# Constant products inside TensorE's waits, in a four-stage transformer kernel

## The chip, the cores and the metric

The kernel runs on one core of a Trainium2 chip. The metric is the device time of one execution in microseconds. Engines are named as in the profile: PE is TensorE (PEld its weight loads), DVE is VectorE, ACT is ScalarE, POOL is GpSimd, SP is SyncE, which issues DMAs.

## The reference

A batch of 8 sequences of 256 rows of 256 numbers runs through four residual layers, each on a layer-normalised input, each weighted by a tanh gate:

1. Cross attention to 120 context rows, 16 heads of 16 (`softmax(q k / 4) v`, then an output projection), with a padding mask.
2. "Mixture attention": 16 heads of 64 attend over the 256 rows. Values and output projection come from 8 experts, of which a gate picks 2 for each head and row.
3. Cross attention again, other weights, with an additive mask of 256 x 120.
4. A mixture of 12 experts with 3 chosen for each row: `gelu(x Wup + bup) Wdown + bdown`, hidden size 1024, summed with softmaxed gate weights.

## The kernel before, in words

Everything is computed to nearly fp32 precision: a number is split into a high and a low fp16 part, and a product is three fp16 products (hi·hi, hi·lo, lo·hi) that add up in PSUM, which is `matmul3` (lines 77 to 85, so most PE rows of the profile carry L82, L83 or L84). Every engine has its program written out in order; semaphores tie them. There are six blocks one after the other (setup, attention 1, mixture attention, attention 2, route, experts), and each ends for all engines before the next begins.

In an attention block (`xattn_stage`) a batch has five front parts, each in the one "front" bank of PSUM: transpose the rows (XN_T, line 517), transpose the context (CTX_T, line 522), project queries (Q_T), keys (K_T) and values (V_). ACT and DVE bring each part to SBUF (high part, then low part), and PE's next part waits for the bank (`front_done`). After that the batch has 8 units of 4 heads: PE scores (a mask product of 128x480 on line 547, in attention 2 three more for the additive mask on line 545, then six products on 32 rows on line 550), DVE maxima, ACT exponentials, PE transposes (line 560), ACT and DVE split them, PE multiplies with V. In the loop the front parts of the next batch stand between the units of this one, and the work on finished rows of the batch before (lines 581, 587, 590) as well. For batch 0 the five front parts stand alone ahead of the loop, and its first two units directly behind them.

The mixture attention (`ffn_stage`) is built in the same way: 16 front parts in two banks, in the order FF_ORDER, alone for batch 0; then 16 heads per batch. After the heads of a batch, ACT and DVE write the head outputs, SP sends them to DRAM and back in another layout, DVE spreads the gate masks, and PE mixes the experts (`mixed_back`, 64 products on line 1208) and multiplies with the output weights (`back_product`). For the last batch nothing is left beside that: the loop's last round, b = B, is this tail.

In the route (`route`) PE transposes the rows, computes gate scores, waits for DVE's choice, ranks and counts (lines 1690 to 1695), transposes gate weights, builds a table of slots from one-hot products (line 1709) and in between the bias term (`base_part`, line 1670), whose last parts wait for DVE. The experts (`run_experts`) begin with two transposes of gathered rows (`turn_rows`, line 1910) and the first up projection (`up(0, 0, 0)`), and go on with 35 blocks.

The lines below are those ahead of which the change puts something: line 595 (`project(0, j)` in the attention), 1221 (the same in the mixture), the two calls at MIX_STEPS and PRODUCT_STEPS, the waits for `masks_made` and `sel_ready` in the route, the end of the route, and `up(0, 0, 0)`.

Of the kernel before, what the change touches and what calls it, by code (L numbers as in the profile page):

```python
# [25 lines left out]
P = 128  # L26
# [9 lines left out]
B, SQ, D = 8, 256, 256  # L36
# [41 lines left out]
def matmul3(pe, out, terms):  # L78

    last = None  # L80
    for n, (lhs, rhs) in enumerate(terms):
        pe.matmul(out, lhs[0], rhs[0], start=(n == 0), stop=False)  # L82
        pe.matmul(out, lhs[0], rhs[1], start=False, stop=False)  # L83
        last = pe.matmul(out, lhs[1], rhs[0], start=False, stop=(n == len(terms) - 1))  # L84
    return last


def rsqrt_all(dve, chain, s):
# [252 lines left out]
ROWS32 = 32  # L341
HG = 4
BACK = 2 * TPB


def xattn_stage(nc, a, s, layer):
# [3 lines left out]
    with ExitStack() as ctx:  # L350
# [24 lines left out]
        ps = ctx.enter_context(nc.psum_tensor(t + "ps", [P, 8, 512], F32))  # L375
# [131 lines left out]
        def _(pe):  # L507
# [84 lines left out]
                last.then_inc(back_ready, 1)  # L592

            for j in range(XA_FRONT):
                project(0, j)
            pe.wait_ge(ones_set, 4)
            score(0, 0)
# [22 lines left out]
        def _(dve):  # L620
# [129 lines left out]
F_XN, F_GATES, F_PV, F_Q, F_K, F_MIXV = "xn", "gates", "pv", "q", "k", "v"  # L750
FF_ORDER = ((F_XN, 0), (F_GATES, 0), (F_PV, 0), (F_PV, 1), (F_Q, 0), (F_K, 0), (F_Q, 1), (F_K, 1), (F_Q, 2), (F_K, 2),
            (F_Q, 3), (F_MIXV, 0), (F_MIXV, 1), (F_MIXV, 2), (F_MIXV, 3), (F_K, 3))
# [3 lines left out]
MIX_STEPS, SPLIT_STEPS, PRODUCT_STEPS, UPDATE_STEPS = [9, 12], [10, 13], [11, 14], [12, 15]  # L756
F_Z, F_OUT = "z", "out"
LOW_KINDS = (F_PV, F_Q, F_K, F_MIXV)


def bank_uses():
# [36 lines left out]
def ffn_stage(nc, a, s):  # L798
# [7 lines left out]
    with ExitStack() as ctx:  # L806
# [293 lines left out]
        def _(pe):  # L1100
# [112 lines left out]
            def back_product(b, ti):  # L1213
                out = open_bank((b, (F_OUT, ti)))
                pe.wait_ge(z_done, TPB * b + ti + 1)
                matmul3(pe, out[:, 0:D],
                        [(tuple(zt[:, hl, ec, :] for hl in range(2)), tuple(s.fo[:, hl, ec, :] for hl in range(2)))
                         for ec in range(E0 // 2)]).then_inc(front_ready, 1)

            for j in range(FF_FRONT):  # L1220
                project(0, j)
            score(0, 0)
            score(0, 1)
            for b in range(B + 1):
                for h in range(H):
                    earlier(b, h, 1, transposes)
                    earlier(b, h, FF_LAG, times_v)
                    if b < B - 1:
                        project(b + 1, h)
                    if b < B and h + 2 < H:  # L1230
                        score(b, h + 2)
                    elif b < B - 1 and h + 2 >= H:
                        score(b + 1, h + 2 - H)
                    for ti in range(TPB):
                        if b >= 1 and h == MIX_STEPS[ti]:
                            mixed_back(b - 1, ti)
                        if b >= 1 and h == PRODUCT_STEPS[ti]:
                            back_product(b - 1, ti)

        @block.vector  # L1240
# [181 lines left out]
UP_PAIRS = M // 2  # L1422
# [120 lines left out]
def route(nc, s, t, sem, ps, xt, xg, rows_in, row_of, expert_of, weights, ident16, out):  # L1543
# [14 lines left out]
    with ExitStack() as prep:  # L1558
# [95 lines left out]
        @block.tensor  # L1654
        def _(pe):
            def gate(k):
                pe.wait_ge(tr_done, k + 1)
                for ti in range(TPB):
                    last = matmul3(pe, G[:, TPB * k + ti, :],
                                   [(tuple(xt[k % 2][:, hl, c, ti * P:(ti + 1) * P] for hl in range(2)),  # L1660
                                     tuple(s.wg[:, hl, c, :] for hl in range(2))) for c in range(C)])
                last.then_inc(gate_done, 1)

            def base_part(q):
                pe.wait_ge(cwt_done, 3 if q == 3 else q // 2 + 1)
                if BASE_BANKS[q] in BASE_BANKS[:q]:
                    pe.wait_ge(b_done, BASE_BANKS.index(BASE_BANKS[q]) + 1)
                for ti in range(TPB):
                    tile = TPB * q + ti
                    last = pe.matmul(BASE(q)[:, ti, :], cwt[:, tile * P:(tile + 1) * P], s.bdown[:], start=True, stop=True)  # L1670
                last.then_inc(b_ready, 1)

            pe.wait_ge(masks_made, 1)
            for k in range(B):
                pe.wait_ge(xn_split, k + 1)
                if k >= 2:
                    pe.wait_ge(tr_done, k - 1)
                for hl in range(2):
                    for c in range(C):
                        for ti in range(TPB):  # L1680
                            at = (hl * C + c) * SQ + ti * P
                            last = pe.transpose(tr(k)[:, at:at + P], limbs[:, TPB * k + ti, hl, c * P:(c + 1) * P], ident16[:])
                last.then_inc(tr_ready, 1)
                if k >= 1:
                    gate(k - 1)
            gate(B - 1)

            pe.wait_ge(masks_made, 6)
            pe.wait_ge(sel_ready, 1)
            pe.matmul(RANK, before[:], sel16[:], start=True, stop=False)  # L1690
            for tile in range(TILES - 1):
                pe.matmul(RANK[:, tile + 1:, :], ones[:], bcast_mid(sel16[:, tile, :], TILES - 1 - tile),
                          start=False, stop=(tile == TILES - 2))
            for tile in range(TILES):
                last = pe.matmul(TOTAL, ones[:], sel16[:, tile, :], start=(tile == 0), stop=(tile == TILES - 1))
            last.then_inc(counted, 1)
            pe.wait_ge(cw_ready, 1)
            for q in range(TILES // 4):
                if q >= 2:
                    pe.wait_ge(cwt_done, q - 1)  # L1700
                for ti in range(4):
                    last = pe.transpose(CW_T(q)[:, ti * P:(ti + 1) * P], cw_out[:, 4 * q + ti, :], s.ident[:])
                last.then_inc(cwt_ready, 1)
            for q in range(BASE_AHEAD):
                base_part(q)
            for n in range(CHOICES):
                if n % TILES == 0:
                    pe.wait_ge(hot_ready, n // TILES + 1)
                last = pe.matmul(MAP, lane_hot[:, n, :], column_hot[:, n, :], start=(n == 0), stop=(n == CHOICES - 1))
            last.then_inc(map_ready, 1)  # L1710
            for q in range(BASE_AHEAD, B):
                base_part(q)

        def lo_part(dve, k):
            tiles = slice(TPB * k, TPB * k + TPB)
# [89 lines left out]
def run_experts(nc, s, t, sem, ctx, ps, xg, xt, rows_in, row_of, ident16, out, weights):  # L1805
# [89 lines left out]
    @block.tensor  # L1895
    def _(pe):
        pe.sem_inc(u_ready, 2 * UP_PAIRS)
        pe.sem_inc(y_ready, 2 * TPB)
        pe.sem_inc(turned, 2)

        def turn_rows(j, par, turn):
            pe.wait_ge(x_loaded[j % RING], 16 * TPB * (j // RING + 1))
            if j >= 1:
                pe.wait_ge(xt_split, j)
            rows = xg[j % RING][:].bitcast(F16)
            for hl in range(2):
                for c in range(C):
                    for ti in range(TPB):
                        at = (hl * C + c) * BT + ti * P
                        last = pe.transpose(T[:, at:at + P], rows[:, ti, hl * D + c * P:hl * D + (c + 1) * P], ident16[:])  # L1910
            last.then_inc(turned, 1)

        def up(j, par, turn):
            pe.wait_ge(up_split, 2 + j + 1)
            pe.wait_ge(xt_split, j + 1)
            for q in range(UP_PAIRS):
                pe.wait_ge(h_gelu, UP_PAIRS * j + q + 1)
                for m in (2 * q, 2 * q + 1):
                    last = matmul3(pe, U(q)[:, m % 2, :],
                                   [(tuple(weights.us[par][:, hl, k, m * P:(m + 1) * P] for hl in range(2)),  # L1920
                                     tuple(xt[par][:, hl, k, :] for hl in range(2))) for k in range(C)])
                last.then_inc(u_ready, 1)

        def down(j, par, turn):
            pe.wait_ge(h_done, UP_PAIRS * (j + 2))
            pe.wait_ge(down_split, 2 + j + 1)
            for ti in range(TPB):
                pe.wait_ge(y_done, TPB * j + ti + 1)
                matmul3(pe, Y(ti),
                        [(tuple(hs[par][:, hl, m, ti * P:(ti + 1) * P] for hl in range(2)),  # L1930
                          tuple(weights.dsp[par][:, hl, m, :] for hl in range(2))) for m in range(M)]).then_inc(y_ready, 1)

        turn_rows(0, 0, 0)
        turn_rows(1, 1, 0)
        up(0, 0, 0)

        def slot(j, par, turn):
            ahead(j, par, turn, 1, up)
            ahead(j, par, turn, 2, turn_rows)
            down(j, par, turn)  # L1940

        for j in range(NB):
            slot(j, j % 2, j // 2)
# [131 lines left out]
```

## Time and profile before

| | us |
|---|---|
| three timed runs | 1438.38, 1441.53, 1442.84 |
| median | 1441.53 |
| span of the profiled execution | 1442.0 |
| PE busy | 1253.7 (87%) |
| PE weight loads | 996.9 (69%) |
| DVE busy | 1135.6 (79%) |
| ACT busy | 903.7 (63%) |
| mean granted clock of TensorE | 0.919 of full speed |

Busy time is the share of the span in which an engine had an instruction under way. The granted clock has two levels: 1.00 is 2.4 GHz, 0.50 is 1.2 GHz, and a number between them is a stretch that holds both. A row of a timeline gives start and duration in us, engine, line and operation, what it writes and reads, and in brackets how long the engine stood idle before it and what ended that. Matmuls are pipelined: a row's duration is longer than the distance to the next row. The stages lie in the span thus: setup to 48.7 us, attention 1 to 255.9, mixture attention to 751, attention 2 to 982.6, route to 1040, experts to the end.

### The profile page before, as it was taken

The page shows a single profiled execution, that of the slowest core. Times are in us where ns is not written, and L with a number is a line of the kernel's source. Part 1 is how long each engine was busy: PE and PEld are TensorE (multiplying, and loading weights), DVE is VectorE, ACT ScalarE, POOL GpSimd, SP SyncE. Part 2 cuts the span into 40 slices and gives each one's busy share as a digit, 9 for nine tenths or more (in the row PEclk, how much of TensorE's full clock was granted, in tenths as well). Part 3 has the DMA queues.
Part 4 walks back from the last instruction along what each step waited for, and adds up shares of the span by engine and source line. Part 5 has one row for each costly group of instructions (what it writes and reads, how often), then busy time and mean ns, then how long its engine had stood idle before and what let it go on. Part 6 is the DMA issues. An engine that isn't in the chain of part 4 may idle for free. (4 is left out here: it accounts for less than half of the span.)

```text
span 1442.0 us, 35263 instructions
## 1 busy us (share of the span) xinstructions
PE 1253.7 (87%) x13822; PEld 996.9 (69%) x13822; DVE 1135.6 (79%) x2068; ACT 903.7 (63%) x2071; POOL 278.4 (19%) x242
## 2 busy tenths in 40 slices
PE   1599998589989899889938999994699999999996
PEld 1376666367767767667725676763489999899995
DVE  5578887689999999999643777777688888888884
ACT  1477875158667677667624667663277677677762
POOL 2000000100000000000000000000236666666663
PEclk8689999799999999999666999995599999999998
DMA  8000000133452353352220000000867788778871
GB/s 231 12 9 9 6 2 2 41 93 74 114 146 67 101 151 76 100 151 73 68 66 9 5 9 5 2 2 1 290 225 227 227 249 245 222 231 250 234 189 30
DMA packets 172065, 152.96 MB, mean 106 GB/s; under 512 B 62589, under 2 KB 154386, under 8 KB 171906
## 3 DMA queue, kind: packets, MB, share of 16 engines
q1 hardware_dynamic: 151906, 129.51, 30.0%
q0 software_dynamic: 13936, 16.79, 6.1%
q10 hardware_dynamic: 6064, 4.46, 1.1%
q8 instruction: 110, 1.80, 0.5%
q14 instruction: 49, 0.40, 0.1%
HBM read 116.89 MB, written 36.70 MB: 107 GB/s over the span
## 5 line engine op out<-in xcount | busy, mean ns | idle before, releaser
L1857 POOL DMA_INDIRECT out<-m_yo,m_xg x70 | 161.5, 2307 | 135.9 <-DVE m_yo L1972 120.5
L1879 ACT ACTIVATE m_hf<-m_ps,m_bue 128x256 f32<-128x256 f32 x280 | 117.3, 471 | 106.5 <-PE m_ps L84 106.5
L82 PE MATMUL m_ps<-m_xt,m_us 128*128 128x256 f16 x560 | 153.7, 274 | 0.0
L83 PE MATMUL m_ps<-m_xt,m_us 128*128 128x256 f16 x560 | 153.7, 274 | 0.0
L84 PE MATMUL m_ps<-m_xt,m_us 128*128 128x256 f16 x560 | 153.6, 274 | 0.0
L82 PE MATMUL m_ps<-m_ds,m_hs 128*128 128x256 f16 x560 | 152.6, 273 | 0.3 <-DVE m_yo L1972 0.3
L84 PE MATMUL m_ps<-m_ds,m_hs 128*128 128x256 f16 x560 | 152.6, 273 | 0.0
L83 PE MATMUL m_ps<-m_ds,m_hs 128*128 128x256 f16 x560 | 152.6, 273 | 0.0
L473 ACT ACTIVATE x_pr<-x_ps,x_mx 128x120 f32<-128x120 f32 x512 | 143.3, 375 | 9.8 <-DVE x_mx L687 9.2
L1053 ACT ACTIVATE f_pr<-f_ps,f_nb 128x256 f32<-128x256 f32 x256 | 107.8, 477 | 66.0 <-DVE f_nb L1331 65.7
L481 ACT ACTIVATE x_pt<-x_ps 120x512 f16<-120x512 f32 x128 | 77.0, 602 | 86.2 <-PE x_ps L84 78.8
L691 DVE SCALAR_TENSOR_TENSOR x_pt<-x_ps,x_pt 120x512 f16<-120x512 f32 x128 | 88.2, 689 | 54.2 <-ACT x_pt L481 53.2
L1539 DVE SCALAR_TENSOR_TENSOR m_ds<-m_draw,m_ds 128x2048 f16<-128x2048 f32 x35 | 80.2, 2292 | 42.7 <-ACT m_ds L1527 42.7
L550 PE MATMUL x_ps<-x_km,x_qt 32*128 32x240 f16 x768 | 105.9, 273 | 0.0
L1335 DVE SCALAR_TENSOR_TENSOR f_pt<-f_ps,f_pt 128x512 f16<-128x512 f32 x128 | 87.5, 684 | 19.9 <-ACT f_pt L1023 19.8
L1962 DVE SCALAR_TENSOR_TENSOR m_hs<-m_hf,m_hs 128x512 f16<-128x512 f32 x140 | 96.9, 692 | 4.8
L550 PEld LDWEIGHTS x_ps<-x_km,x_qt 32*128 32x128 f16 x768 | 63.6, 96 | 53.0 <-issue 46.3
L1486 POOL DMA_INDIRECT m_xg<-expert_in,m_row_of x70 | 83.2, 1189 | 69.6 <-DVE m_row_of L1796 40.8
L82 PE MATMUL f_ps<-f_kt,f_qt 64*128 64x256 f16 x256 | 72.0, 282 | 25.5 <-ACT f_pr L1053 25.3
L1023 ACT ACTIVATE f_pt<-f_ps 128x512 f16<-128x512 f32 x128 | 79.0, 617 | 23.7 <-PE f_ps L84 23.5
L687 DVE TENSOR_REDUCE x_mx<-x_ps 128x4 f32<-128x480 f32 x128 | 83.5, 653 | 12.3 <-PE x_ps L550 9.8
L1331 DVE TENSOR_REDUCE f_nb<-f_ps 128x2 f32<-128x512 f32 x128 | 87.6, 685 | 2.0 <-PE f_ps L84 0.7
(367 smaller groups left out, 3832.7 us busy)
## 6 DMA issues: line engine op xcount, KB each, us to landing
m_uraw<-in_L_ffn_Wup SPq DMA_DIRECT2D x35, 1024.0 KB, 5.5
m_draw<-in_L_ffn_Wdown SPq DMA_DIRECT2D x35, 1024.0 KB, 5.8
head_values<-f_v_row SPq DMA_DIRECT2D x16, 520.0 KB, 5.5
f_vh<-head_values SPq DMA_DIRECT2D x16, 520.0 KB, 3.9
head_outputs<-f_at_row SPq DMA_DIRECT2D x16, 512.0 KB, 3.0
f_at_in_t<-head_outputs SPq DMA_DIRECT2D x16, 512.0 KB, 6.1
expert_values<-f_pv_row SPq DMA_DIRECT2D x8, 512.0 KB, 2.8
f_pv_in_t<-expert_values SPq DMA_DIRECT2D x8, 512.0 KB, 5.6
```

The source lines that it names most:

```text
L82: pe.matmul(out, lhs[0], rhs[0], start=(n == 0), stop=False)
L83: pe.matmul(out, lhs[0], rhs[1], start=False, stop=False)
L84: last = pe.matmul(out, lhs[1], rhs[0], start=False, stop=(n == len(terms) - 1))
L473: ins = act.activation(pr[u % 2][:, h, :], S(u)[:, h, :], ACT.Exp, bias=mx[u % 2][:, h:h + 1])
L550: last = pe.matmul(S(u)[:, 2 * m:2 * m + 2, :], qt[par][rows, ql, m, ti * P:ti * P + P], km[par][rows, kl, m, :, :], start=False, stop=(m ...
L691: dve.scalar_tensor_tensor(pt[u % 2][:, 1], PT(u), SPLIT, pt[u % 2][:, 0], ALU.mult, ALU.subtract).then_inc(pt_done, 1)
L1053: ins = act.activation(pr[h % 2][:, ti, :], S(h)[:, ti, :], ACT.Exp, bias=nb[h % 2][:, ti:ti + 1])
L1331: dve.tensor_reduce(nb[h % 2][:], S(h), AX_X, ALU.max, negate=True).then_inc(s_max, 1)
L1335: dve.scalar_tensor_tensor(pt[h % 2][:, 1].rearrange("p c t q -> p (c t q)"), PT(h), SPLIT, pt[h % 2][:, 0].rearrange("p c t q -> p (c t q)"),
L1857: pool.indirect_dma_start(rows_of, bass.IndirectOffsetOnAxis(xg[j % RING][:, ti, D:D + 1].bitcast(I32), 0), yo[j % 2][:, ti, :], None, bou ...
L1879: ins = act.activation(hf[:, q, m, :], U(q)[:, m, :], ACT.Gelu, bias=weights.bue[par][:, 2 * q + m:2 * q + m + 1], scale=UNSPLIT)
L1962: dve.scalar_tensor_tensor(hs[par][:, 1, 2 * q:2 * q + 2, :], hf[:, q], SPLIT, hs[par][:, 0, 2 * q:2 * q + 2, :], ALU.mult, ALU.subtract). ...
```

## The change

A helper issues `n` products of 128x512 fp16 elements of the mixture attention's query weights with a 128x128 piece of the same weights, into a bank of PSUM that nothing reads before it is written anew. They wait for nothing and tell no semaphore. The helper is called ahead of each front part of batch 0 in both attentions and of four parts in the mixture attention, three times in the mixture's last round (`b == B`), twice in the route and once in the experts: 153 products in all. At the route's end a wait for `map_done` goes ahead of them, because their bank held the slot table.

```diff
+def idle_products(pe, s, bank, n):
+    for _ in range(n):
+        pe.matmul(bank, s.fq[:, 0, 0, 0:P], s.fq[:, 0, 0, 0:512], start=True, stop=True)
...
+XA_IDLE = (3, 5, 2, 6, 4)
...
             for j in range(XA_FRONT):
+                idle_products(pe, s, ps[:, 7, :], XA_IDLE[j])
                 project(0, j)
...
+FF_IDLE = {(F_XN, 0): 2, (F_GATES, 0): 4, (F_K, 0): 3, (F_MIXV, 0): 14}
...
             for j in range(FF_FRONT):
+                idle_products(pe, s, ps[:, 7, :], FF_IDLE.get(FF_ORDER[j], 0))
                 project(0, j)
...
                         if b >= 1 and h == MIX_STEPS[ti]:
+                            if b == B and ti == 0:
+                                idle_products(pe, s, ps[:, 2, :], 40)
                             mixed_back(b - 1, ti)
                         if b >= 1 and h == PRODUCT_STEPS[ti]:
+                            if b == B:
+                                idle_products(pe, s, ps[:, 2, :], 4)
                             back_product(b - 1, ti)
...
             gate(B - 1)
+            idle_products(pe, s, ps[:, 7, :], 20)
             pe.wait_ge(masks_made, 6)
             pe.wait_ge(sel_ready, 1)
...
             for q in range(BASE_AHEAD, B):
                 base_part(q)
+            pe.wait_ge(map_done, 1)
+            idle_products(pe, s, ps[:, 7, :], 16)
...
         turn_rows(0, 0, 0)
         turn_rows(1, 1, 0)
+        idle_products(pe, s, ps[:, UP_PAIRS + 2, :], 6)
         up(0, 0, 0)
```

PE's order at the start of attention 1, before the change (x_xn are the rows, x_ctx the context, x_ps the attention's PSUM):

```order
L506 UNCONDITIONAL_BRANCH
L517 MATMUL x_ps<-ident,x_xn 128x128 x4
L522 MATMUL x_ps<-ident,x_ctx 128x120 x2
L82 MATMUL x_ps<-x_xt,w_q 128x256
L83 MATMUL x_ps<-x_xt,w_q 128x256
```

And with the change (lines below the helper are numbered 6 or 7 higher; fq are the constant weights):

```order
L513 UNCONDITIONAL_BRANCH
L91 MATMUL x_ps<-fq 128x512 x3
L524 MATMUL x_ps<-ident,x_xn 128x128 x4
L91 MATMUL x_ps<-fq 128x512 x5
L529 MATMUL x_ps<-ident,x_ctx 128x120 x2
L91 MATMUL x_ps<-fq 128x512 x2
L82 MATMUL x_ps<-x_xt,w_q 128x256
L83 MATMUL x_ps<-x_xt,w_q 128x256
```

Nothing has changed places; the constant products stand between two parts, ahead of the wait of the second. The start of attention 2 reads the same.

PE's order in the tail of the mixture attention with the change, from the last product with values (f_vh) on; before it, the same rows stand without those of L91:

```order
L84 MATMUL f_ps<-f_vh,f_pt 128x65
L91 MATMUL f_ps<-fq 128x512 x40
L1217 MATMUL f_ps<-f_spread_z,f_at_in_t 64x4x16 x64
L91 MATMUL f_ps<-fq 128x512 x4
L82 MATMUL f_ps<-fo,f_zt 128x256
```

The 40 follow the last head directly, ahead of the mixing's waits for the masks and for the head outputs; 4 stand between each mixing and the output product that waits for its split.

PE's order from the slot table (m_lane_hot) over the route's end into the experts, with the change; the two branches end one block and begin the next:

```order
L1724 MATMUL m_ps<-m_ds,m_lane_hot 128x70 x48
L1684 MATMUL m_ps<-bdown,m_cwt 128x256 x8
L91 MATMUL m_ps<-fq 128x512 x16
L1572 UNCONDITIONAL_BRANCH
L1912 UNCONDITIONAL_BRANCH
L1927 MATMUL m_ps<-m_ident,m_xg 128x128 x16
L91 MATMUL m_ps<-fq 128x512 x6
L82 MATMUL m_ps<-m_xt,m_us 128x256
```

Sixteen are the last that PE does in the route; six stand between the two row turns (x16 together) and the first up projection.

## Rows read from the trace of the kernel before

**Rows 1.** Stretches: us, busy time and instructions of each engine, granted clock (PEclk), DMA.
```profile
58.20:61.60 3.40, 0.80 (x12) 0.64 (x12) 0.69 (x1) 1.78 (x6) 0.00 (x0) 1.00 0.00 0
61.70:82.10 20.40, 19.61 (x99) 12.40 (x100) 9.69 (x20) 10.38 (x30) 0.00 (x0) 0.50 0.03 8
686.30:706.50 20.20, 19.89 (x138) 14.20 (x137) 13.20 (x20) 13.14 (x33) 0.00 (x0) 0.50 0.40 112
713.00:724.90 11.90, 10.49 (x202) 9.17 (x200) 8.84 (x19) 8.45 (x26) 0.00 (x0) 1.00 0.01 1
735.80:744.30 8.50, 6.45 (x140) 5.15 (x140) 1.78 (x4) 1.09 (x2) 0.00 (x0) 0.50 0.12 32
751.10:785.20 34.10, 25.51 (x104) 14.52 (x105) 11.09 (x27) 9.86 (x27) 1.19 (x6) 0.50 0.08 17
796.60:947.40 150.80, 150.80 (x1585) 106.74 (x1584) 112.52 (x246) 104.23 (x313) 0.00 (x0) 1.00 0.02 5
1040.00:1048.10 8.10, 6.30 (x37) 4.80 (x38) 3.13 (x4) 4.17 (x5) 3.00 (x2) 0.50 0.84 310
...
37.80:44.50 6.70, 4.26 (x31) 3.04 (x29) 1.00 0.00 0
```
**Rows 2.** Stretches, line 1183 alone (128x512 products): us, PE, PEld, clock, DMA.
```profile
302.00:303.60 1.60, 1.46 (x6) 0.54 (x6) 1.00 0.03 3
307.20:309.90 2.70, 2.60 (x6) 0.71 (x6) 0.54 0.00 0
```
**Rows 3.** Stretches, tile x_xt alone: query projections of batch 0 and 1.
```profile
55.00:58.00 3.00, 2.74 (x12) 1.64 (x12) 0.00 (x0) 0.00 (x0) 0.50 0.19 52
97.80:99.40 1.60, 1.47 (x12) 1.10 (x12) 0.00 (x0) 0.00 (x0) 1.00 0.33 90
```
**Rows 4.** Timeline of PE, front of attention 1: start, us, instruction, idle before.
```profile
53.52 0.66 PE L522 MATMUL x_ps<-ident,x_ctx 120*128 120x120 f32 x2 [2.63 <-DVE x_xt L656]
55.09 0.39 PE L82 MATMUL x_ps<-x_xt,w_q 128*128 128x256 f16 x1 [0.91 <-DVE x_ct L660]
...
60.22 0.23 PE L82 MATMUL x_ps<-x_ct,w_k 128*128 128x120 f16 x1 [2.39 <-DVE x_qt L665]
```
**Rows 5.** Timeline of PE, first units of batches 0, 1, 2, both attentions.
```profile
63.85 0.58 PE L547 MATMUL x_ps<-x_mb,mask_w 128*128 128x480 bf16 x1
...
88.03 0.36 PE L547 MATMUL x_ps<-x_mb,mask_w 128*128 128x480 bf16 x1 [0.20 <-ACT x_pr L473]
...
110.49 0.36 PE L547 MATMUL x_ps<-x_mb,mask_w 128*128 128x480 bf16 x1 [0.43 <-ACT x_pr L473]
...
768.08 0.61 PE L547 MATMUL x_ps<-x_mb,mask_w 128*128 128x480 bf16 x1
...
796.57 0.36 PE L547 MATMUL x_ps<-x_mb,mask_w 128*128 128x480 bf16 x1
...
821.71 0.36 PE L547 MATMUL x_ps<-x_mb,mask_w 128*128 128x480 bf16 x1
```
**Rows 6.** Timeline of PE, front of the mixture: gate projection, first value products.
```profile
259.86 0.39 PE L82 MATMUL f_ps<-fg,f_xt 128*128 128x256 f16 x1 [1.91 <-DVE f_xt L1273]
...
287.07 0.23 PE L82 MATMUL f_ps<-f_pv_in_t,f_spread_v 128*128 128x64 f16 x1 [5.30 <-DVE f_spread_v L1304]
```
**Rows 7.** Timeline of PE, tail of the mixture: first mixing, first output product.
```profile
735.77 0.45 PE L1208 MATMUL f_ps<-f_spread_z,f_at_in_t 128*64 128x64 f16 x9 [10.82 <-issue]
...
739.20 0.37 PE L82 MATMUL f_ps<-fo,f_zt 128*128 128x256 f16 x1 [1.50 <-DVE f_zt L1348]
```
**Rows 8.** Stretches, line 1208 alone: a mixing at either clock.
```profile
715.50:716.80 1.30, 1.20 (x64) 1.09 (x64) 1.00 0.00 0
735.70:737.80 2.10, 1.92 (x64) 1.82 (x64) 0.50 0.54 145
```
**Rows 9.** Timeline of PE: ranking in the route, first row turn of the experts.
```profile
1007.86 0.32 PE L1690 MATMUL m_ps<-m_sel,m_before 128*128 128x192 f16 x1 [8.26 <-DVE m_sel L1752]
...
1040.60 0.69 PE L1910 MATMUL m_ps<-m_ident,m_xg 128*128 128x128 f16 x5 [7.64 <-PEq L1558]
```

## The prediction

> **What bounds the kernel now.** I read the granted clock first, stretch by stretch, then the products that stand on both sides of a clock change, then the waits of TensorE. The first view splits the span into stretches at TensorE's upper level (2.4 GHz, shown as 1.00) and at its lower one (1.2 GHz, shown as 0.50) [rows 1]. The reader is to see two kinds of low stretch. In 61.7–82.1, 686.3–706.5 and 768–785 PE is busy nearly all the time at 0.50: there the clock is the limit. In the others (the fronts of the stages, the tail of the mixture attention, the start of the experts) PE mostly waits, and its short bursts run at 0.50 and stand on the chain between two waits. The same product at both levels gives the price of a level: six of 128x512 take 1.46 us at 1.00 and 2.60 at 0.54 [rows 2], so one costs 0.22 to 0.24 us high and 0.43 low; the twelve products of a query projection take 1.47 against 2.74 [rows 3]. The third view shows what ends PE's waits: evacuations by DVE in the fronts, 2.63, 0.91 and 2.39 us long in the first attention [rows 4], and larger ones further on [rows 6 to 8].
>
> **The change part by part.** It takes nothing away and moves no wait. It adds 153 products of 128x512 on 128 rows, each ahead of a wait of PE. Each costs nothing where it ends before its wait does; what it can give is a high clock for what follows.
>
> First batch of attention 1. In PE's order stand 3, 5, 2, 6 and 4 products ahead of the five parts. At the low price 5 take 2.13 us against the 2.63 of wait, 2 take 0.85 against 0.91, 6 take 2.56 against 2.39, or 1.3 if the clock has risen [rows 2, 4]. So they fit. With the real work between, PE is nearly never idle from the stage's first wait to the query projection. In the trace the clock was high from 58.2 on, right after the 12 query products had run without a break, and fell again when PE was busy 0.80 of the next 3.40 us [rows 1]. I take it as high before the query projection: 2.74 becomes 1.47, −1.27 on the chain. Then the units. From the first unit of batch 0 to the first of batch 1 it is 24.18 us, from there to batch 2 22.46 [rows 5], although batch 0 has none of the work on finished rows. At the high clock batch 0 takes no more than a steady batch, −1.7; the bounds are 0 (the clock falls as before) and half of PE's 19.61 busy us at 0.50, −9.8 [rows 1], which ACT and DVE will not allow. I take −1.7, the end next to a row, because the first units wait for exponentials and their scores run on 32 rows: the clock may fall there. Attention 1: −3.0.
>
> Front of the mixture. The gate projection is again 12 products of 256 columns after a wait of 1.91 us, which 4 low products (1.7) fill [rows 2, 6]: −1.27. The first value products follow a wait of 5.30 us [rows 6]; 14 products take 3.1 us high, 6.0 low (0.7 too long). The 48 value products that ran at 0.50 there would go from some 3.2 us (287.1 to 290.3 in the trace) to about half, −1.4, but DVE's spreads stand between them. The 2 ahead of the transposes and the 3 ahead of the first keys last 0.9 and 1.3 us at most, low; if no wait covered them they would cost that, +2.2. Of +2.2 to −2.7 I take −2.0: the first term whole, the second by half.
>
> Tail of the mixture. 40 products go into the wait of 10.82 us ahead of the last mixing [rows 7]. The clock is high just before (713–724.9, [rows 1]), so they take 8.8 us and end 2 us before the wait does. Behind them, the 64 mixing products take 1.20 us instead of 1.92, twice [rows 8], and the twelve of the output 1.47 instead of 2.74, with 4 products (0.9) inside the 1.50 us wait [rows 3, 7]: −0.72·2 −1.27 = −2.7, all of it on the chain, since nothing else runs. If the clock is low when they start they take 17.2 us: 6.4 too long.
>
> First batch of attention 2. The front has the same five waits, and its query and key products both ran low (751.1–785.2 is at 0.50 throughout, [rows 1]): −1.27, and for the key's 12 products of 120 columns, by columns, 0.6. The units: 28.49 us for batch 0, 25.14 for batch 1 [rows 5]. In the steady batches PE is busy 150.80 of 150.80 us at 1.00 [rows 1], so PE's work alone sets the pace, and here every unit holds three more full-width products of 128 rows (line 545) than in attention 1, enough to keep PE busy from the first unit on. As long as a steady batch: −3.35. At most half of PE's busy time from 768.1 to 785.2 comes back, −8.5. Batch 0 lacks the work on finished rows and the tail of a batch before, so I go well past the first bound: −7.0. Attention 2: −8.9.
>
> Route and experts. 20 products precede the ranking, after a wait of 8.26 us [rows 9]: 8.6 low, 4.9 high, and the clock rises on the way; DVE is at other work until after the totals anyway. 16 more follow at PE's end of the route, in 7.64 us of idle before the experts [rows 9]; 6.9 low, so they fit. In the experts' start PE is busy 6.30 of 8.10 us at 0.50 [rows 1]. Half of that comes back, −3.15, but the 6 products ahead of the first up projection stand behind row turns whose next step waits for nothing, so they are paid in full, 1.3: −1.85. If the clock is low there they cost 2.6 and give nothing. From there PE runs without a break, so whatever is won stays won.
>
> Sum: −3.0 −2.0 −2.7 −8.9 −1.85 = −18.5 on the profiled span of 1442.0, 1423.5. The median of the runs shown is 1441.53, 0.5 less: 1423.
>
> **A rule against the row.** Much of the first units is fp32 transposes. In 37.8–44.5 the clock is 1.00, and all that PE had done before and does in it is transposes of line 247 [rows 1]. So they do raise it. The Trainium skill, "TensorE: Matmul & The Clock Gate", section "Part 4: PE-mode transpose", says that transposes do not count as PE activity for the clock in the same way. By that rule the first batches would lose the clock between projections, and the sum would be that of case (a); the trace speaks against it.
> The same page, section "Back-to-back issue gap", gives some 0.13 us per 512-column product in a stream. An estimate by it: the 40 products would end 5.6 us before the tail's wait does, long enough for the clock to fall as it did in the trace, and 2.7 us of the sum would go (1426). The row shows 0.22 to 0.24 [rows 2], and by the row only 2 us stay open.
>
> **The rivals.** (a) The fronts speed up but the clock does not hold through the units of either first batch, as it did not in 61.7–82.1, where PE was busy 19.61 of 20.40 us at 0.50 [rows 1]: being busy alone did not raise it there, with 32-row scores and fp32 transposes (that transposes alone are to blame has 0.03 of this case's chance). Left are −1.27, −2.0, −2.7, −1.9, −1.85 = −9.7: 1432. Against it for attention 2: the same mixture holds 1.00 for 150 us.
> (b) Nothing changes: the waits are set by DVE, ACT and DMAs, and bursts that end earlier only wait longer. For it: every wait of rows 4 is ended by DVE. Against it: the evacuations wait for PE in turn. 1441.
> (c) Slower: constant operands do not raise the clock, and all 153 products run at 0.43. Its place is the tail, 17.2 us in a wait of 10.82: +6.4; then 2.6 ahead of the experts, 0.7 at the value products, 0.2 each at the two output products. +10: 1452. It decides from the point where the 40 products take over 0.27 us each. For it: at 686.3–706.5 PE is busy all along at 0.50, 20 us before the tail, and if that stretch lies later the tail starts low. Against it: the mixing before the tail brought the clock back in the trace.
>
> **How the numbers follow.** Forecast 0.68; (a) 0.17; (b) 0.07; (c) 0.08. Each end has a few us of luck in where the clock falls: between the two ends of the units' gain the forecast case alone runs from 1414 to 1430. The 8-in-10 range takes in (a): 1413 to 1435. A measurement here tells about 0.3% (4.3 us) from no change. Faster by more than that: the forecast, (a) and little else, 0.85; within: 0.08; slower: 0.07.
>
> **What would show it.** In the profile after: the query projections of both attentions in 1.5 us; the first batch of attention 2 in 20 to 22 us at clock 1.00 (wrong if 28); that of attention 1 in 21 to 23, and in 24 if its clock falls; the 40 products of 0.22 us each, over before the last mixing starts, which takes 1.2; the first up projection at 1.00 from its start, 0.4 us later than now after the row turns. The prediction fails if the first batch of attention 2 stays at 0.50, or if the last mixing follows the 40 products without a wait.

## The result and the profile after

The changed kernel takes 1422.24 us (median of 4 runs, 1418.0 to 1424.71) against 1440.12 (4 runs, 1438.38 to 1442.84): ratio 0.9872, 95% interval 0.9845 to 0.99. Measured a second time it was 1420.31 against 1440.12, ratio 0.9862 (0.9837 to 0.9887). The profiled execution has a span of 1423.0 us where before had 1442.0.

The page of the kernel after, engine totals: the added products make PE busier, and the span is shorter all the same.

```profile
span 1423.0 us, 35569 instructions
...
PE 1272.8 (89%) x13975; PEld 1001.2 (70%) x13975; DVE 1135.9 (80%) x2068; ACT 903.0 (63%) x2071; POOL 280.4 (20%) x242
```

Stretches of the kernel after (us, busy time and instructions of PE, PEld, DVE, ACT, POOL, granted clock, DMA), the counterpart of [rows 1]:

```profile
51.60:65.20 13.60, 9.40 (x64) 5.21 (x63) 5.93 (x16) 4.94 (x14) 0.00 (x0) 1.00 0.06 16
65.30:75.50 10.20, 10.20 (x45) 6.26 (x44) 4.05 (x7) 5.33 (x17) 0.00 (x0) 0.50 0.05 14
174.60:181.30 6.70, 6.70 (x51) 4.83 (x50) 5.18 (x13) 3.96 (x12) 0.00 (x0) 0.50 0.00 0
281.00:283.70 2.70, 0.63 (x22) 0.63 (x23) 1.91 (x3) 0.00 (x0) 0.00 (x0) 1.00 0.05 4
283.80:293.90 10.10, 8.23 (x99) 6.46 (x97) 5.86 (x7) 2.99 (x5) 0.00 (x0) 0.50 0.27 63
...
734.30:737.60 3.30, 3.30 (x14) 1.61 (x12) 0.69 (x1) 0.36 (x1) 0.00 (x0) 0.50 0.00 0
760.90:781.50 20.60, 20.60 (x189) 13.55 (x188) 13.39 (x27) 14.59 (x44) 0.00 (x0) 1.00 0.03 9
1021.10:1038.60 17.50, 14.47 (x128) 11.57 (x127) 10.01 (x13) 10.68 (x18) 3.01 (x2) 1.00 0.63 224
```

Attention 2's first batch is at 1.00 from end to end, and so is the start of the experts. Attention 1's first batch begins at 1.00 and falls at 65.3, in the units. Two places of the mixture behind added products are at 0.50 as well: the value products behind 281.0–283.7, where PE worked 0.63 of 2.70 us, and an output product of the tail.

Timeline of PE in the kernel after, the front of attention 1 (start, us, instruction, idle before), against [rows 4]:

```profile
48.80 1.44 PE L91 MATMUL x_ps<-fq 128*128 128x512 f16 x3 [4.49 <-PEq L138]
...
50.88 1.61 PE L91 MATMUL x_ps<-fq 128*128 128x512 f16 x5
53.58 0.43 PE L529 MATMUL x_ps<-ident,x_ctx 120*128 120x120 f32 x2 [1.08 <-DVE x_xt L664]
53.84 0.60 PE L91 MATMUL x_ps<-fq 128*128 128x512 f16 x2
54.91 0.28 PE L82 MATMUL x_ps<-x_xt,w_q 128*128 128x256 f16 x1 [0.47 <-DVE x_ct L668]
...
56.23 1.46 PE L91 MATMUL x_ps<-fq 128*128 128x512 f16 x6
58.78 0.23 PE L82 MATMUL x_ps<-x_ct,w_k 128*128 128x120 f16 x1 [1.09 <-DVE x_qt L673]
```

Four of the five groups end before their wait does: 1.08, 0.47 and 1.09 us of idle remain of 2.63, 0.91 and 2.39, and 0.60 of 1.47 ahead of the value projection. The first group doesn't: DVE had the rows ready at 49.68 (49.66 before the change), and the transposes follow the 3 products without idle at 50.03, where they began at 49.81; some 0.2 us are lost there. The query products last from 54.91 to the 6 constant ones at 56.23.

First units of batches 0, 1 and 2 in both attentions, kernel after, against [rows 5]:

```profile
62.41 0.36 PE L554 MATMUL x_ps<-x_mb,mask_w 128*128 128x480 bf16 x1 [0.49 <-issue]
83.73 0.36 PE L554 MATMUL x_ps<-x_mb,mask_w 128*128 128x480 bf16 x1 [0.21 <-ACT x_pr L480]
106.18 0.36 PE L554 MATMUL x_ps<-x_mb,mask_w 128*128 128x480 bf16 x1 [0.42 <-ACT x_pr L480]
...
760.92 0.36 PE L554 MATMUL x_ps<-x_mb,mask_w 128*128 128x480 bf16 x1
781.52 0.36 PE L554 MATMUL x_ps<-x_mb,mask_w 128*128 128x480 bf16 x1
806.66 0.36 PE L554 MATMUL x_ps<-x_mb,mask_w 128*128 128x480 bf16 x1
```

Batch 0 takes 21.32 us in attention 1 (before 24.18) and 20.60 in attention 2 (before 28.49), less than the next batches with 22.45 and 25.14.

The mixture's tail and the start of the experts, kernel after, against [rows 7, 9]:

```profile
721.72 8.80 PE L91 MATMUL f_ps<-fq 128*128 128x512 f16 x40
732.82 1.20 PE L1217 MATMUL f_ps<-f_spread_z,f_at_in_t 128*64 128x64 f16 x64 [2.30 <-issue]
733.95 1.61 PE L91 MATMUL f_ps<-fq 128*128 128x512 f16 x4
735.53 0.37 PE L82 MATMUL f_ps<-fo,f_zt 128*128 128x256 f16 x1
...
737.97 1.20 PE L1217 MATMUL f_ps<-f_spread_z,f_at_in_t 128*64 128x64 f16 x64
739.10 1.04 PE L91 MATMUL f_ps<-fq 128*128 128x512 f16 x4
740.75 0.27 PE L82 MATMUL f_ps<-fo,f_zt 128*128 128x256 f16 x1 [0.61 <-DVE f_zt L1362]
...
1024.41 0.61 PE L1927 MATMUL m_ps<-m_ident,m_xg 128*128 128x128 f16 x8 [1.83 <-PEq L1572]
1026.22 0.61 PE L1927 MATMUL m_ps<-m_ident,m_xg 128*128 128x128 f16 x8 [1.21 <-ACT m_xt L1889]
1026.67 1.46 PE L91 MATMUL m_ps<-fq 128*128 128x512 f16 x6
1027.96 0.27 PE L82 MATMUL m_ps<-m_xt,m_us 128*128 128x256 f16 x1
```

The 40 take 0.22 us each and leave 2.30 us of the wait. Both mixings take 1.20, but the first output product runs from 735.53 to 737.97, since the clock is at 0.50 there.

Where the time went, from such rows in two profiles of each kernel. A line is the length of a stretch, from start to start; "the other batches" run to the last mask product, and the last head, the tail and the up products are counted to the end of their last product.

| stretch | before | again | after | again |
|---|---|---|---|---|
| start to attention 1's first mask product | 63.85 | 63.75 | 62.41 | 61.83 |
| attention 1, batch 0 | 24.18 | 24.14 | 21.33 | 21.45 |
| attention 1, the other batches | 150.28 | 150.21 | 152.72 | 150.23 |
| mixture, row transposes to the seventh head's scores | 56.46 | 56.24 | 55.13 | 55.08 |
| mixture, fifth to last head of the last batch | 35.46 | 33.57 | 34.01 | 34.65 |
| mixture, tail after the last values | 21.86 | 21.62 | 20.33 | 19.24 |
| attention 2, row transposes to first mask product | 16.00 | 15.52 | 13.23 | 13.11 |
| attention 2, batch 0 | 28.49 | 28.40 | 20.61 | 20.60 |
| attention 2, the other batches | 170.01 | 169.98 | 170.00 | 169.98 |
| route to first row turn | 55.23 | 55.12 | 54.94 | 54.57 |
| first row turn to first up product | 3.02 | 3.02 | 3.55 | 3.55 |
| first 96 up products | 12.84 | 12.44 | 10.64 | 10.64 |

Attention 2's two lines hold 10.65 of the 19.0 us between the first profiles.

### The profile page after: what moved, and what is told of

Read it like the earlier page. It is cut to its first block and busy times, and to the rows that moved or that the text cites. A ratio compares the mean times of both kernels' runs of the same rounds, so it can differ in the third digit from the quotient of the medians.

```text
span 1423.0 us, 35569 instructions
## 1 busy us (share of the span) xinstructions
PE 1272.8 (89%) x13975; PEld 1001.2 (70%) x13975; DVE 1135.9 (80%) x2068; ACT 903.0 (63%) x2071; POOL 280.4 (20%) x242
## 5 line engine op out<-in xcount | busy, mean ns | idle before, releaser
L557 PE MATMUL x_ps<-x_km,x_qt 32*128 32x240 f16 x768 | 102.6, 267 | 0.0
```

What stands on the lines that cost most here:

```text
L557: last = pe.matmul(S(u)[:, 2 * m:2 * m + 2, :], qt[par][rows, ql, m, ti * P:ti * P + P], km[par][rows, kl, m, :, :], start=False, stop=(m ...
```

## The experiments

My theory: what a group is worth is the level of the clock in the work behind it, and what raises the level is how much of the array works. Rivals: any unbroken work of PE would do, or the groups lean on each other. The edits are to the changed kernel, except that of `attention2_alone`, which adds the helper and one group to the kernel before. `after_again`, `before_again` and the second execution of `without_attention2` run a kernel once more as it was. Every stage is read from one profile of each run.

**Attention 2's products alone** (`attention2_alone`).

```diff
+XA_IDLE = (3, 5, 2, 6, 4)
...
             for j in range(XA_FRONT):
+                if layer == 1:
+                    idle_products(pe, s, ps[:, 7, :], XA_IDLE[j])
                 project(0, j)
```

> Only the 20 products of the second attention are left; the other 133 and the wait for map_done are out. Theory (each group is worth what the higher clock gives to the work behind it, and the groups add): from the first transposes of attention 2 to its first mask product 13.2 us (before 16.0), batch 0 20.6 us (before 28.5), so 10.6 us under the kernel before: 1429.5. The mixture's tail and the start of the experts stay as before. Rival (the groups lean on each other, a stage starts high only because the one before it ended high): attention 2 stays at 0.50 or gains at most the projections, 1437 or more.

1427.58 us against 1441.08, ratio 0.9906 (0.9881 to 0.9932). Its first batch of attention 2, 763.13 to 783.74:

```profile
763.10:783.70 20.60, 20.60 (x189) 13.55 (x188) 13.38 (x27) 14.57 (x44) 0.00 (x0) 1.00 0.03 8
```

13.40 us of front and 20.61 of batch 0, as forecast, although the mixture's tail ahead of it stayed at 21.64. The group stands on its own; the rival falls. The median is 13.5 us lower where these two stretches give 10.5; the runs reach from 1424.96 to 1433.04.

**All but attention 2's** (`without_attention2`, and the same kernel once more).

```diff
-                idle_products(pe, s, ps[:, 7, :], XA_IDLE[j])
+                if layer == 0:
+                    idle_products(pe, s, ps[:, 7, :], XA_IDLE[j])
```

> The changed kernel without the 20 products of attention 2. Theory (the groups add): attention 2 as before the change, 16.0 us of front and 28.5 us of batch 0 at 0.50, so 10.7 us over the changed kernel: 1433. Rival (the work before, or the better tail of the mixture, brings the clock up anyway): batch 0 of attention 2 under 24 us and 1426 or less.

1426.28 us against 1441.08 (1420.98 to 1430.81), ratio 0.9904 (0.9883 to 0.9926). That is 4 to 6 us over the changed kernel (its two medians), not 10.7. In the profile the front of attention 2 ran low and took 15.86 us, but batch 0 took 21.09, at a mean clock of 0.97: it came up about 1 us after the first units began.

```profile
755.90:777.00 21.10, 21.10 (x189) 13.66 (x188) 13.50 (x27) 14.56 (x44) 0.00 (x0) 0.97 0.04 9
```

So:

> The changed kernel without attention 2's products, a second time: in the first profile batch 0 of attention 2 took 21.1 us, its clock up from the first units though its front ran at 0.50. Theory (at 0.50 these units lie at the edge, and what the clock does is settled anew in each execution): another value this time, up to 28.5 us. Rival (the groups ahead of attention 2 bring this about): 21.1 us again.

The stretches of that second execution, from the end of the front on:

```profile
754.70:771.70 17.00, 15.25 (x55) 7.80 (x56) 6.83 (x16) 6.36 (x19) 0.00 (x0) 0.50 0.03 9
771.80:788.20 16.40, 16.40 (x173) 11.36 (x170) 11.01 (x22) 11.90 (x35) 0.00 (x0) 1.00 0.01 2
```

Here batch 0 began at 758.97, stayed low until 771.8 and took 26.54 us (one run, 1431.11). The same program, the same stage: 21.09 and 26.54. So attention 2 can get part of the gain without its own products. Front and batch 0 together took 36.95 and 41.89 us against 33.84 in the changed kernel, 3.1 and 8.1 more, mean 5.6, near the 4 to 6 us of the medians; two executions don't tell how often either happens.

**The kernel before, again** (`before_again`).

> The kernel before a second time, for its first batches. Theory (below the edge it stays low every time): attention 1's batch 0 24.2 us, attention 2's 28.5 us, the first up projections 12.8 us. Rival (the clock comes up by itself in some executions): one of them at least 3 us shorter.

1439.81 us (one run). Batch 0 24.14 and 28.40, the up products 12.44; in attention 2:

```profile
761.30:781.60 20.30, 19.12 (x72) 10.49 (x73) 8.13 (x18) 6.45 (x18) 0.00 (x0) 0.50 0.03 8
```

Low again. Attention 2's batch 0 took 20.60 or 20.61 us in all eight profiles with 128-row products ahead of it. Without them it ran low for some 17 us in both profiles of before and in `rows32`, and for 13 us or 1 in those of `without_attention2`. Whether that difference is chance or comes from the groups ahead stays open; three against two executions don't settle it.

**The same products on 32 rows** (`rows32`).

```diff
-        pe.matmul(bank, s.fq[:, 0, 0, 0:P], s.fq[:, 0, 0, 0:512], start=True, stop=True)
+        pe.matmul(bank, s.fq[0:32, 0, 0, 0:P], s.fq[0:32, 0, 0, 0:512], start=True, stop=True)
```

> The same 153 products with operands on 32 of the 128 rows: the same columns and the same number of instructions, in the same places. Theory (what counts is how much of the array works, so that PE busy with 32 rows does not bring the clock up): attention 2 stays at 0.50, batch 0 takes 28 us, the first up projections 12.8; the products fill waits and gain nothing, and those that do not fit cost up to 5 us: 1440 to 1446. Rival (any unbroken work of PE brings the clock up): as the changed kernel, 1422, with batch 0 of attention 2 in 20.6 us at 1.00.

1450.44 us against 1441.08, ratio 1.0058 (1.0037 to 1.0079): 9 us slower than before, and 28 to 30 over the kernel with the same instructions on 128 rows. The stretches of the mixture's front, of the tail, of attention 2's front (two) and of its first units, and two rows of the tail:

```profile
267.00:290.80 23.80, 16.62 (x113) 10.14 (x111) 15.89 (x24) 6.04 (x11) 2.35 (x6) 1.00 0.26 61
727.80:748.20 20.40, 20.40 (x157) 9.10 (x155) 6.34 (x8) 1.77 (x3) 0.00 (x0) 0.50 0.33 104
755.10:765.30 10.20, 9.29 (x30) 3.73 (x30) 2.56 (x10) 1.26 (x3) 1.28 (x6) 0.50 0.18 41
765.40:768.70 3.30, 2.52 (x21) 1.24 (x20) 0.69 (x1) 1.68 (x6) 0.00 (x0) 1.00 0.00 0
768.80:789.20 20.40, 19.67 (x74) 10.51 (x73) 8.17 (x18) 6.46 (x19) 0.00 (x0) 0.50 0.03 8
```

```profile
725.61 15.12 PE L91 MATMUL f_ps<-fq 32*128 32x512 f16 x40
740.66 1.92 PE L1217 MATMUL f_ps<-f_spread_z,f_at_in_t 128*64 128x64 f16 x64
```

In 727.8–748.2, the 40 products and the tail behind them, PE worked 20.40 of 20.40 us and stayed at 0.50; in the front of attention 2, 9.29 of 10.20 and the same. From 765.4 to 768.7, behind the query projection, the clock was up, and then low again through the first units; the front of `before_again` does this without any added product (757.8–761.1 at 1.00). So PE busy nearly all along with products on 32 rows didn't bring attention 2's batch 0 up, which took 28.38 us; any unbroken work of PE is not enough. The clock even fell under the 40 products, which began at 1.00: they took 15.12 us and the tail 26.09 (+4.2). With the row turns (+2.8), attention 1's batch 0 (25.72, +1.5) and its other batches (152.76, +2.5) that is more than I had forecast. One stretch doesn't fit "gain nothing": the mixture's front took 54.28 us, 2.0 to 2.2 less than the 56.24 to 56.46 without products, its clock up from 267.0 to 290.8, where before it fell under the first keys (269.9–273.2 at 0.50). With 128 rows it took 52.70 to 55.13. What the 32 rows did there, one profile doesn't settle. Only 32 and 128 rows were run, on the same weights: that the share of the array at work decides is read from these two points.

**One late group** (`late12`).

```diff
+                idle_products(pe, s, ps[:, 7, :], (XA_IDLE, (0, 0, 0, 0, 12))[layer][j])
```

> In attention 2 alone the five groups (3, 5, 2, 6, 4) become one of 12, ahead of the value projection; all else as in the changed kernel. Theory (the units need only a high clock at their start and then hold it themselves): the front goes back to 0.50 and 16 us, and the 12 products, 5.1 us at 0.43, outlast the wait of 1.9 us by up to 3.2; but batch 0 takes 20.6 us at 1.00: 1426 to 1429. Rival (the units need the whole front high): batch 0 stays near 28.5 us at 0.50 and the 3.2 us are lost: 1436 to 1439.

1423.54 us against 1441.08, ratio 0.989 (0.9856 to 0.9925).

```profile
752.96 3.85 PE L91 MATMUL x_ps<-fq 128*128 128x512 f16 x12
...
757.31 0.77 PE L552 MATMUL x_ps<-causal_b,ident_b 128*128 128x480 bf16 x3
```

```profile
741.60:755.00 13.40, 7.70 (x35) 4.58 (x36) 3.22 (x8) 3.14 (x8) 0.45 (x3) 0.50 0.13 31
755.20:778.50 23.30, 23.30 (x205) 15.15 (x204) 14.35 (x29) 15.69 (x46) 0.00 (x0) 1.00 0.03 8
62.40:79.80 17.40, 16.14 (x165) 11.54 (x165) 12.97 (x26) 14.11 (x44) 0.00 (x0) 1.00 0.04 9
```

The front takes 16.25 us (+3.0), batch 0 of attention 2 20.61: a clock that is high at the start of the units is enough, and they hold it. (In `without_attention2` it was low at their start and came up a little later.) Twelve products in one place give 7.6 of attention 2's 10.65 us. The median lies 2.5 us below the forecast. In the profiled execution attention 1 also held its clock (last line), and its batch 0 took 17.39 us; the runs reach from 1418.79 to 1434.71, and the others aren't profiled.

**The changed kernel again** (`after_again`).

> The changed kernel a second time, unaltered, for what differs between executions of one program. Theory (where the clock is raised by a margin it comes up every time, and where the work itself is near the edge it differs): attention 2's batch 0 again in 20.6 us; attention 1's batch 0 in 17.4 us if the clock holds through its units and 21.3 if it falls as in the first profile; 1418 to 1425. Rival (the clock follows the program alone): every stage within 0.3 us of the first profile.

1420.31 us against 1440.12, ratio 0.9862 (0.9837 to 0.9887). Attention 2 within 0.12 us in both lines; attention 1's clock fell again, at 63.3, 1.5 us behind the first mask product where it was 2.9 in the first profile:

```profile
61.80:63.20 1.40, 1.38 (x9) 0.72 (x10) 0.98 (x3) 0.00 (x0) 0.00 (x0) 1.00 0.00 0
63.30:73.50 10.20, 10.20 (x45) 6.53 (x44) 5.44 (x11) 5.17 (x16) 0.00 (x0) 0.50 0.05 14
```

The tail was 19.24 us this time, with its output product at 1.00, and attention 1's other batches 150.23 for 152.72. So stretches of one program differ by 1 to 2.5 us between these two executions; attention 2's first batch no longer does.

**Without the six** (`no_six`).

```diff
-        idle_products(pe, s, ps[:, UP_PAIRS + 2, :], 6)
```

> The changed kernel without the 6 products ahead of the first up projection. Theory (the 16 products at the end of the route have raised the clock already, and the 6 are paid in full): the first 96 up products still take 10.6 us at 1.00 and start 1.1 to 1.4 us sooner after the second row turn: 1421. Rival (the clock falls in the two waits around the row turns without them): 12.8 us as before the change, 1424.

1420.2 us against 1440.12, ratio 0.9857 (0.9831 to 0.9883); the timing can't tell it from the changed kernel, the trace can:

```profile
1022.21 0.61 PE L1927 MATMUL m_ps<-m_ident,m_xg 128*128 128x128 f16 x8 [1.91 <-PEq L1572]
1024.02 0.61 PE L1927 MATMUL m_ps<-m_ident,m_xg 128*128 128x128 f16 x8 [1.21 <-ACT m_xt L1889]
1024.46 0.27 PE L82 MATMUL m_ps<-m_xt,m_us 128*128 128x256 f16 x1
```

From the first row turn to the first up product 2.25 us (with the six 3.55), and the 96 up products take 10.64 either way. The 16 at the end of the route had raised the clock; the six cost 1.3 us and gave nothing.

**The last batch of the mixture** (`last_batch`). Two products for each of seven heads, at the place where the clock fell in every profile so far. `bank_left` makes PE wait until the bank's last contents have been read.

```diff
+            def last_idle(b, h):
+                if b == B - 1 and 2 <= h <= 8:
+                    bank_left((b, FF_ORDER[-1]))
+                    idle_products(pe, s, bank((b, FF_ORDER[-1])), 1)
...
+                    last_idle(b, h)
                     earlier(b, h, FF_LAG, times_v)
+                    last_idle(b, h)
```

> The changed kernel with two more constant products for each of seven heads (h = 2 to 8) in the mixture's last batch, where the clock fell to 0.50 for 17 us in the profile after and 24 us before. Theory (a head at 0.50 takes 3.09 us of PE, at 1.00 1.75, DVE needs about 2.0; 14 products cost at most 14 x 0.22 = 3 us, mostly inside waits): about eight heads at 2.1 us in place of 3.1, 1414 to 1416. Rival (PE is the limit at either level and the products are paid on top, or the clock falls anyway): 1422 to 1427.

1416.85 us against 1440.12, ratio 0.9841 (0.9819 to 0.9862). The stretch from the fifth to the last head, changed kernel first, this one second:

```profile
682.00:715.90 33.90, 30.99 (x389) 23.98 (x388) 21.97 (x38) 22.52 (x62) 0.00 (x0) 0.75 0.30 80
```

```profile
677.00:705.40 28.40, 26.02 (x402) 19.73 (x401) 21.81 (x38) 22.51 (x62) 0.00 (x0) 1.00 0.33 85
```

At 1.00 throughout, 28.48 us for 34.01: −5.5, a little less than forecast. In all ten profiles without these products the clock fell here (33.57 to 35.46 us); in the three with them, this one, `fill_last` and `best`, it held (28.48 to 29.00). The median is 3.5 us under that of `after_again`; the two intervals overlap, so the trace shows this gain and the timing by itself doesn't.

**Filling what was left** (`fill_last`).

```diff
-FF_IDLE = {(F_XN, 0): 2, (F_GATES, 0): 4, (F_K, 0): 3, (F_MIXV, 0): 14}
+FF_IDLE = {(F_XN, 0): 2, (F_GATES, 0): 4, (F_K, 0): 3, (F_MIXV, 0): 22, (F_MIXV, 1): 3, (F_MIXV, 3): 3}
...
-                                idle_products(pe, s, ps[:, 2, :], 40)
+                                idle_products(pe, s, ps[:, 2, :], 49)
...
-                                idle_products(pe, s, ps[:, 2, :], 4)
+                                idle_products(pe, s, ps[:, 2, :], 6)
```

> As last_batch, and the waits left open are filled: 49 products for 40 in the mixture's tail, 6 for 4 ahead of its two output products, 22 for 14 ahead of the first value products, 3 ahead of the second and the fourth group of them. Theory: the clock no longer falls in the tail, where one output product took 2.51 us for 1.47 (-1.0), nor at the value products, where 72 products and the keys took 7.4 us for 4.1 (up to -3, less what DVE holds back): 2 to 3 us under last_batch, 1412. Rival (DVE sets the pace there): no less than last_batch.

1418.34 us against 1440.12, ratio 0.9854 (0.9832 to 0.9875): no gain over `last_batch`, a miss. The tail took 19.04 us where `last_batch` had 19.21 and `after_again` 19.24 without the filling. The value products now ran at 1.00,

```profile
281.50:292.00 10.50, 8.77 (x131) 5.60 (x131) 7.72 (x9) 2.67 (x5) 0.00 (x0) 1.00 0.28 62
```

and the mixture's front took 52.94 us, against 53.95 in `last_batch`; but 52.70 in `no_six`, which had the 14 of the changed kernel. One profile each doesn't carry a difference of this size. The whole profile is 4.0 us longer than that of `last_batch`, and 3.9 of it is attention 1's batch 0, the same code in both: 21.27 us, where its clock fell, and 17.40, where it held.

**The best of them** (`best`): `last_batch` without the six, and in attention 1's first batch

```diff
+            if layer == 0:
+                idle_products(pe, s, ps[:, 7, :], 2)
             pe.wait_ge(ones_set, 4)
             score(0, 0)
...
+                    if layer == 0 and b == 0 and u < 3:
+                        idle_products(pe, s, ps[:, 7, :], (2, 1, 1)[u])
                     if b < B - 1 and u < XA_FRONT:
```

> last_batch, without the 6 products ahead of the first up projection, and with 6 more in attention 1's first batch: 2 ahead of the first scores, 2, 1 and 1 in its units 0 to 2, where the clock fell in four of seven profiles that had it high before the first unit. Theory (each of these is worth its own row): -1.3 for the 6; batch 0 of attention 1 at 1.00 throughout, 17.4 + 4 x 0.2 = 18.2 us for a mean of 19.8: 1413 to 1416. Rival (the time that attention 1 wins is given back in its later batches, where the clock falls once as often as not, and the products are paid on top): 1416 to 1418.

1413.22 us (1411.42 to 1418.14) against 1440.01, ratio 0.9822 (0.9804 to 0.984).

```profile
62.30:79.90 17.60, 16.83 (x168) 11.92 (x169) 12.94 (x26) 14.11 (x44) 0.00 (x0) 1.00 0.04 9
```

Batch 0 of attention 1 takes 17.63 us at 1.00. That the 6 products did this isn't shown by one profile: three of the eight that have the changed kernel's front and none of these 6 held the clock as well (17.38 to 17.40). The rival is half right: the other batches took 152.90, and 152.57 to 152.61 in the three other profiles whose batch 0 held the clock, against 150.2 or 150.3 in six of the nine profiles where it didn't. So 2.4 to 2.7 us were lost in four of four and in three of nine; whether that is chance stays open. The ratio's interval lies below that of the changed kernel's first measurement (0.9845 to 0.99) and overlaps that of its second, and that of `last_batch`.

## Why the prediction was right, point by point

The time, 1422.24 and 1420.31 for 1423, and the mechanism were right; the terms less evenly.

- Attention 2, −8.9: −10.65 and, in the second profiles, −10.2 (16.00 + 28.49 to 13.23 + 20.61, and 15.52 + 28.40 to 13.11 + 20.60). The units gave 7.9 and 7.8 for 7.0, the front 2.8 and 2.4 for 1.9. Right, and a little small: beside the two projections the value products and the first three products of the additive mask ran at 1.00 too (these three 0.77 us for 1.38).
- Attention 1, −3.0: −4.3 up to batch 1 in the first profile (1.4 + 2.9), of which 2.4 was lost again in a later batch; −4.6 in the second (1.9 + 2.7), with nothing lost. The front was right (1.27 forecast). The step that failed is "at the high clock batch 0 takes no more than a steady batch, −1.7": held at 1.00 it takes 17.4 us (`late12`), 5 under a steady batch, so the gain is 1.6 to 2.9 where the clock falls (22.62 in `no_six`, 21.33) and 6.8 where it holds. I had set the work that batch 0 lacks into attention 2's term and not into this one. That the clock may fall there, I had right. In the eight profiles with the changed kernel's front here, batch 0 took 17.38 to 22.62 us, falling in five.
- Front of the mixture, −2.0: −1.3 and −1.2 (second profiles 56.24 and 55.08). The gate projection gave its 1.3; in these two profiles the clock fell at the value products, in the rest of the wait. In the seven profiles with this front unchanged it took 52.70 to 55.13 us, mean 53.97, against 56.24 to 56.46 in three without products: −2.35 on average. So the −2.0 was of the right size, and the two profiles above are the two smallest gains.
- Tail, −2.7: −1.5 and −2.4. "By the row only 2 us stay open" was right on the time (2.30, at 0.22 us a product) and wrong on what follows: the clock fell behind it, at 734.3, and the first output product took 2.51 us where it takes 1.47 at 1.00. In the second profile the clock didn't fall.
- Route and experts, −1.85: −2.0 and −1.8 (0.3 + 2.2 − 0.5, and 0.55 + 1.8 − 0.5). The six are paid, 1.3 as forecast (`no_six`); without them the gain is 3.3 and 3.1, so "half of 6.30", 3.15, was of the right size.
- Stretches that the change doesn't touch, taken as 0: +0.7 us in sum in the first profiles. That these nearly cancel is luck, and so is part of the total: the attentions gave 3.0 us more than forecast up to their second batches, and the mixture's front and tail 1.9 less.

Of the rivals, (a) came true for attention 1's clock, not for its price. (b) is out, by the time and by the rows. (c), a high clock that the products don't bring, is nearest to what 32 rows give. Its 1452 and the 1450.44 agree in part by luck: the tail lost 4.2 us and not 6.4, and 2.5 of the rest came from attention 1's other batches, which (c) doesn't name. The prediction named constant operands as the reason; it didn't ask how many rows the products use, and that is what made the difference, with the same constant weights.

The Trainium skill, "TensorE: Matmul & The Clock Gate", section "Part 4: PE-mode transpose", has it that transposes don't count as work of PE for the clock in the same way. By that rule the units of both first batches would have lost the clock. Attention 2's held it with the transposes in it (760.9–781.5 at 1.00); this case gives no sign that the rule set the time. The last line of [rows 1], on which the prediction leans as well, is line 247 alone; of the 33 products in 37.8–44.5 two are of lines 251 and 252, and they are transposes too. Why attention 1's clock falls in five of eight executions and holds in three stays open.

## What to carry to other kernels

Constant products inside a wait pay where long work at the lower clock follows them and keeps the clock by itself: look for stretches where the matrix engine is busy all the time at half clock, and put the products right ahead of those (twelve gave most of what twenty did). Here products on all 128 rows did it and products on 32 didn't; nothing between was run. They should end before the wait does, and six that followed work which had raised the clock already were only paid for. Where the work doesn't keep the clock, as in the mixture's last batch, a few products inside it can. Compare several profiles of one program before reading a difference of a few us as an effect: attention 1's first batch took 17.4 to 22.6 us in eight executions of the same code.

## What the runs showed of the hardware

- PE busy 20.40 of 20.40 us, some 15 us of it with products on 32 rows, stayed at 0.50 (`rows32`), and 40 products of 512 columns on 32 rows that began at 1.00 fell on the way (15.12 us for 8.80).
- The same work can run at either level for long: attention 2's first batch took 20.6 us in eight of eight profiles in which it began high, and 28.4 to 28.5 in three that began low; in two others that began low the clock came up on the way (21.09 and 26.54). The mixture's last batch doesn't hold the upper level by itself (33.6 to 35.5 us from its fifth head on, ten profiles); with two products for each of seven heads it does (28.5 to 29.0, three profiles).
- When the clock changes isn't fixed by the program: in eight executions of one attention front and its first batch, it fell in five, at 63.3 and 65.3 in the two of the changed kernel, and not at all in `without_attention2` (the first), `late12` and `last_batch`.
